# A fused attention, gate and routing pipeline: wider softmax-sum pieces, bf16 high parts written by ScalarE, a prefix in three steps, and a second table of places for the last three iterations

## The reference, cut to what matters

```
# x: (16, 128, 32, 32): 16 images of 1024 pixels, 128 channels
xn   = batchnorm(x)                                   # running statistics
qkv  = qkv_w @ xn + qkv_b                             # 4 heads of 32
attn = softmax(q^T k / sqrt(128)) over 1024 keys
x    = x + out_w @ (attn v) + out_b
t    = tokens(x)                                      # (16, 1024, 128)
z    = layernorm(t)
k, v = per-head norm of z (8 heads of 16, std with n-1)
t    = t + z @ (k^T v / N) + z                        # linear attention
z2   = layernorm(t)
p    = softmax(z2 @ gate_w + gate_b); the two largest of 8 experts
t    = t + sum over the two of p_e * (gelu(z2 @ W1_e + b1_e) @ W2_e + b2_e)
out  = images(t)
```

## Time and profile before

| what | value |
|---|---|
| median of 3 runs | 2252.08 us (2238.56 to 2256.55) |
| profiled execution | 2246.34 us, of which the span of instructions 2244.6 us |
| mean granted TensorE clock | 0.863 |
| phase 1 with attention | from 50 us to 1530 us of the span |
| iterations 16 to 18, tables | 1530 us to 1660 us |
| phases 2 and 3 | 1660 us to 2244.6 us |

### The profile page before, as it was taken

The page is one execution under the profiler, slowest core; times in us unless marked ns, Lnnn a source line. Parts: engine busy times, 40 slices in busy tenths (PEclk is TensorE's granted clock), DMA queues, the critical chain, the costliest instruction groups (busy, mean ns, idle before and its releaser), DMA issues.

```text
span 2244.6 us, 38139 instructions
## 1 busy us (share of the span) xinstructions
PE 1754.7 (78%) x11103; PEld 884.2 (39%) x11256; DVE 1379.7 (61%) x3701; ACT 1071.3 (48%) x1898; POOL 1434.8 (64%) x1779
## 2 busy tenths in 40 slices
PE   5999898897888989798898978885337677777744
PEld 2233333332333333333333333333326566566632
DVE  5677878686776768677686866754434333333345
ACT  1565655555455555545455555452115444444432
POOL 1777587875968678596877769676335555555530
PEclk8999999998988999799898999896568888887865
DMA  2220220211202022120202112010323333322259
GB/s 64 57 57 12 55 81 17 76 37 51 77 14 84 15 76 53 38 77 21 76 13 75 47 44 73 6 38 31 101 76 119 107 115 96 93 76 75 74 150 319
DMA packets 130824, 155.20 MB, mean 69 GB/s; under 512 B 19678, under 2 KB 93170, under 8 KB 130688
## 3 DMA queue, kind: packets, MB, share of 16 engines
q1 hardware_dynamic: 113408, 117.76, 18.9%
q0 software_dynamic: 16896, 35.69, 4.7%
q10 hardware_dynamic: 384, 0.00, 0.0%
HBM read 65.03 MB, written 55.84 MB: 54 GB/s over the span
## 4 chain that ended last, share of the span: by engine, by line
PE 49%; issue 14%; DVE 12%; another core or an unknown queue 8%; POOL 6%; ACT 5%; SPq 4%; DMA 1%; DVEq 0%; ACTq 0%; POOLq 0%
PE psum L1573 8%; PE psum L1620 7%; PE psum L1593 7%; PE psum L1683 6%; DVE rowmax L1198 5%; PE psum L1670 5%; PE psum L1554 3%; PE psum L1421 3%; POOL probs L624 2%; PE psum L1428 2%; PE psum L1576 2%; PE psum L1659 2%; PE psum L1458 1%; POOL arena L624 1%
## 5 line engine op out<-in xcount | busy, mean ns | idle before, releaser
L1198 DVE TENSOR_REDUCE rowmax<-psum 128x1 f32<-128x512 f32 x1024 | 670.1, 681 | 304.3 <-PE psum L1620 184.9
L1620 PE MATMUL psum<-arena 128*128 128x512 bf16 x872 | 332.9, 405 | 103.8 <-DVE rowmax L1198 81.1
L797 ACT ACTIVATE probs<-psum 128x1024 f32<-128x1024 f32 x256 | 251.1, 1021 | 209.7 <-PE psum L1576 203.5
L797 ACT ACTIVATE arena<-psum 128x1024 f32<-128x1024 f32 x256 | 252.7, 1021 | 179.8 <-PE psum L1576 176.6
L610 POOL DMA_INDIRECT sorted_scratch<-rows,slot_idx x256 | 251.1, 981 | 91.9 <-issue 69.6
L1620 PEld LDWEIGHTS psum<-arena 128*128 128x128 bf16 x1024 | 92.5, 101 | 550.0 <-DVE rowmax L1198 384.9
L1573 PE MATMUL psum<-qk 32*128 32x512 f32 x2048 | 300.6, 657 | 7.9 <-ACT probs L797 4.3
L1683 PE MATMUL psum<-probs 128*128 x1088 | 186.4, 326 | 100.5 <-ACT probs L866 100.4
L624 POOL TENSOR_TENSOR probs<-probs 128x256 f32<-128x256 f32 x352 | 243.7, 729 | 16.5 <-PE psum L1593 13.5
L624 POOL TENSOR_TENSOR arena<-arena 128x256 f32<-128x256 f32 x352 | 243.9, 728 | 13.5 <-PE psum L1593 10.9
L1683 PEld LDWEIGHTS psum<-probs 128*128 128x128 f32 x1088 | 174.9, 236 | 128.9 <-issue 121.6
(11 more groups left out here) (203 smaller groups left out, 2794.3 us busy)
## 6 DMA issues: line engine op xcount, KB each, us to landing
arena<-part SPq DMA_DIRECT2D x256, 128.0 KB, 2.8
qk<-sorted_scratch SPq DMA_DIRECT2D x136, 144.0 KB
probs<-y_scratch SPq DMA_DIRECT2D x64, 256.0 KB, 5.1
x_in<-in_x_dram SPq DMA_DIRECT2D x16, 512.0 KB, 3.5
x_res<-in_x_dram SPq DMA_DIRECT2D x16, 512.0 KB
t_scratch<-t SPq DMA_DIRECT2D x16, 512.0 KB
arena<-t_scratch SPq DMA_DIRECT2D x8, 1024.0 KB
out_dram<-probs SPq DMA_DIRECT2D x32, 256.0 KB, 5.3
```

Source lines behind the costliest of these rows:

```text
L797: a.activation(group[:, 2 * i:2 * i + 2, :].rearrange("p s n -> p (s n)"), st_pair[i], ACT.Exp, scale=float(C) ** -0.5).then_inc(exp_done, 1)
L1198: v.tensor_reduce(rowmax[:, half, kh, h, j:j + 1], ps[:, :], AX.X, ALU.max)\
L1620: t_.matmul(ps[:, :], qs1[:, par, h, qb * P:(qb + 1) * P], ks1[:, par, h, kh * HALF:(kh + 1) * HALF], start=True, stop=True)\
```

## The change

1. SUM_PARTS goes from 8 to 4: each pair of exponential blocks is added in four instructions of 512 columns, not in eight of 256.
2. The high part of q and k is written by ScalarE from PSUM, ahead of the float32 copy that it already wrote; GpSimd keeps the low part. For image 0, two high parts move from DVE to ScalarE.
3. The Gram matrix's four instructions after PE's product (usum, kvw[0], udiag, kcc) move from DVE to ScalarE, in the piece "gram"; the head mask is multiplied into vrow once at the start, and the identity is added in the second product, so that `kv_product` has one instruction less (three after usum, not four).
4. The running count over blocks is made in three instructions of 64 columns (sums of two, of four, of eight) from padded tiles `chosen`, `two_of`, `four_of`. Two slot products become one instruction, two slot sums too.
5. In AT: zT1 goes from quarter 27 to 24, ss from 25 to 23, the third pair of z from 20 to 19, prefix to (27, 28, 31).
6. Iterations 16 to 18 take their places from a second table, AFTER. Against AT it has, among others: proj1 13, gram 27, usum 31, z (17, 19, 19, 19), ss 23, square 24, heads 27, u 31, scatter (11, 13, 14, 16, 19, 19, 22, 26), z2 (12, 13, 15, 15), ln0 15, ln1 1, norm1 1, kv1 to kv3 at 0, 2, 5, slot_numbers 6, prefix (30, 31, 31), stats0a and stats0b 14, 15, deviations0 18, gsum 19.
7. In the last image's second half only the pairs 0 and 1 are summed by GpSimd; PE takes the blocks of pairs 2 and 3 one by one.

```diff
-    PAIRS, SUM_PARTS = 4, 8
+    PAIRS, SUM_PARTS = 4, 4
     SUMMED = (0, 1, 2, 3)
+    LAST_SUMMED = (0, 1)
+    def summed_at(n):
+        return LAST_SUMMED if n == 2 * B - 1 else SUMMED
+    def table(pair, p):
+        return AT if 2 * pair + p < B else AFTER
...
+        chosen = sb("chosen", [P, 1 + BLK, E])
+        two_of = sb("two_of", [P, 2 + BLK, E])
+        four_of = sb("four_of", [P, 4 + BLK, E])
...
                 pool.wait_ge(raw_ready, 4 * b + c + 1)
-                g.tensor_copy(part[:, 0, which, cols], qk[:, par, which, cols]).then_inc(high_ready, 1)
-                pool.wait_ge(high_ready, parts_made(b, c))
+                pool.wait_ge(high_ready, 4 * b + c + 1)
                 g.tensor_tensor(part[:, 1, which, cols], qk[:, par, which, cols], part[:, 0, which, cols],
                                 ALU.subtract).then_inc(mid_ready, 1)
...
+                    if b > 0 and name == "q0":
+                        for h in range(NH):
+                            act.wait_ge(stacked1[1 - par][h], 16 * STACK1_DMAS * ((b - 1) // 2 + 1))
+                    a.activation(part[:, 0, which, cols], ps[:, :], ACT.Identity,
+                                 bias=bqk[:, which:which + 1]).then_inc(high_ready, 1)
                     a.activation(qk[:, par, which, cols], ps[:, :], ACT.Identity,
                                  bias=bqk[:, which:which + 1]).then_inc(raw_ready, 1)
...
+                elif name == "gram":
+                    ps = from_shared(name, pair, p)
+                    a.activation(usum[:, :], ps[:, C:C + 1], ACT.Copy).then_inc(gram_out, 1)
+                    a.activation(kvw[:, 0, :], ps[:, 0:C], ACT.Copy, scale=kcol[:, 0:1]).then_inc(gram_out, 1)
+                    act.wait_ge(gram_out, 3 * b + 1)
+                    a.activation(udiag[:, :], ident[:, :], ACT.Copy, scale=usum[:, :]).then_inc(udiag_ready, 1)
+                    a.activation(kcc[:, :], usum[:, :], ACT.Identity, scale=kcol[:, 0:1], bias=kb_n[:, :])\
+                     .then_inc(gram_out, 1)
...
-                    v.scalar_tensor_tensor(kvw[:, 3, :], vrow[:, 1, :], kcc[:, :], kvw[:, 2, :],
+                    dve.wait_ge(gram_out, 3 * b + 3)
+                    v.scalar_tensor_tensor(kvw[:, 3, :], vrow[:, 1, :], kcc[:, :], ident[:, :],
                                            ALU.mult, ALU.add).then_inc(kv_step, 1)
                 else:
-                    dve.wait_ge(kv_step, 6 * b + 6)
-                    v.tensor_tensor(kvw[:, 4, :], kvw[:, 3, :], headmask[:, :], ALU.mult).then_inc(bd_ready, 1)
-                    dve.wait_ge(bd_ready, 2 * b + 1)
-                    v.tensor_tensor(bd[:, :], kvw[:, 4, :], ident[:, :], ALU.add).then_inc(bd_ready, 1)
+                    dve.wait_ge(kv_step, 3 * b + 3)
+                    v.tensor_tensor(bd[:, :], kvw[:, 2, :], kvw[:, 3, :], ALU.add).then_inc(bd_ready, 1)
...
+                    if k == 0:
+                        ins = v.tensor_tensor(two_of[:, 2:, :], chosen[:, 1:, :], chosen[:, 0:BLK, :], ALU.add)
+                    elif k == 1:
+                        ins = v.tensor_tensor(four_of[:, 4:, :], two_of[:, 2:, :], two_of[:, 0:BLK, :], ALU.add)
                     else:
-                        dve.wait_ge(prefix_step, 8 * b + k)
-                    v.tensor_tensor(before[:, k + 1, :], before[:, k, :], lg[:, 8, k, :], ALU.add)\
+                        ins = v.tensor_tensor(before[:, 1:, :], four_of[:, 4:, :], four_of[:, 0:BLK, :], ALU.add)
...
-                for c in range(2):
-                    v.tensor_reduce(slot_of[:, c, :], slot[:, 1 + c, :, :], AX.X, ALU.add).then_inc(slot_step, 1)
+                v.tensor_reduce(slot_of[:, :, :], slot[:, 1:3, :, :], AX.X, ALU.add).then_inc(slot_step, 1)
...
                 for i in pairs:
-                    if i in SUMMED:
+                    if i in summed_at(n):
                         pe.wait_ge(summed, len(SUMMED) * n + SUMMED.index(i) + 1)
                     else:
                         pe.wait_ge(probs_used, PAIRS * n + i + 1)
-                    groups = (2 * i,) if i in SUMMED else (2 * i, 2 * i + 1)
+                    groups = (2 * i,) if i in summed_at(n) else (2 * i, 2 * i + 1)
```

More of the change, by code:

```diff
@@ L89, in conv_attention_hybrid_kernel, with order @@
     }
-    SHARED = {n: (AT[n], LAG[n]) for n in LAG}
-    PAIRS, SUM_PARTS = 4, 8
+    AFTER = dict(AT)
+    AFTER.update({'rank': 1, 't2_0': 8, 't2_1': 10, 'proj0': 11, 'proj1': 13, 'z2T0': 17, 'z2T1': 18, 'logits': 19, 'zT0': 23, 'zT1': 24, 'gram': 27, 'usum': 31, 'values1': 1, 'ln1': 1, 'z2': (12, 13, 15, 15), 'gexp': 20, 'ln0': 15, 'z': (17, 19, 19, 19), 'square': 24, 'ln_heads': 26, 'norm1': 1, 'd16': 20, 'u': 31, 'scatter': (11, 13, 14, 16, 19, 19, 22, 26), 'kv1': 0, 'kv2': 2, 'kv3': 5, 'slot_numbers': 6, 'stats1a': 9, 'stats1b': 10, 'deviations1': 13, 'gate': (20, 23, 23, 23, 24, 24, 24, 24, 25, 25, 26, 26, 26, 26, 27, 29), 'prefix': (30, 31, 31), 'stats0a': 14, 'stats0b': 15, 'deviations0': 18, 'gsum': 19, 'ss': 23, 'heads': 27, 'den1': 5})
+    PAIRS, SUM_PARTS = 4, 4
     SUMMED = (0, 1, 2, 3)
-    ORDER = sorted(SHARED, key=lambda n: SHARED[n][0])
+    LAST_SUMMED = (0, 1)
[3 more added lines that the diff above has]
+        return AT if 2 * pair + p < B else AFTER
+    def order(pair, p):
+        return sorted(LAG, key=lambda n: table(pair, p)[n])
     OTHER_WEIGHTS_AT = max(AT[n] for n in ("q0", "k0", "q1", "k1")) + 1
@@ L135, in row_target, with denominators_at @@
         return (0, 1, r) if r < 4 else (1, 0, r - 4) if r < 8 else (1, 1, 0)
-    DENOMINATORS = tuple((SHARED[n][0], SHARED[n][1], int(n[3])) for n in ORDER if n[:3] == "den")
+    def denominators_at(pair, p):
+        return tuple((table(pair, p)[n], LAG[n], int(n[3])) for n in order(pair, p) if n[:3] == "den")
     DEN_STEPS = ((0, (0, 1)), (1, (2, 3)))
@@ L638, in iteration @@
                         for half in (0, 1):
[L639 to L642, removed]
+                            when = 16 * half + at["sum"][i]
+                            lag = -(when // QUARTERS)
+                            if q == when % QUARTERS and in_range(lag, pair, p):
+                                b = image(lag, pair, p)[0]
+                                if i in summed_at(2 * b + half):
+                                    sum_pair(b, half, i)
                     if in_range(1, pair, p):
                         b, _, par = image(1, pair, p)
-                        if q == AT["split"][0]:
+                        if q == at["split"][0]:
                             _, prp, parp = image(0, pair, p)
@@ L1528, in previous @@
             def previous(name, pair, p):
-                mine = ORDER
+                mine = order(pair, p)
                 i = mine.index(name)
@@ L1628, in iteration @@
                             values(b, par, sv, 1 if j == 1 else 0)
-                    for first, lag, half in DENOMINATORS:
+                    for first, lag, half in denominators_at(pair, p):
                         for later, pairs in DEN_STEPS:
```

177 lines of the change are left out of this document (90 added, 87 removed).

## The result

| | before | after |
|---|---|---|
| median of 4 runs each | 2246.77 us (2238.56 to 2256.55) | 2347.59 us (2342.01 to 2350.81) |
| profiled execution, its own time and span | 2246.34, 2244.6 us | 2342.01, 2340.2 us |
| mean granted clock | 0.863 | 0.859 |

The ratio is 1.0444, 95% interval 1.0392 to 1.0497: 101 us slower, where 2247 us had been forecast with a range of 2213 to 2283.

A forecast was written before the change was run, and what follows sets the result against it. Steady iterations were taken as bound by TensorE's work plus stalls, the tail by engine-to-engine latencies. Terms +24 - 17 + 0 - 10 = -3 us against 2246.3 gave 2243; forecast median 2247, range 2213 to 2283.

The forecast's parts named there:

- sums of 512 columns: GpSimd's pair sums over VectorE's chain in quarter 17: each later chain instruction waits 0.6 us more; +24 us, 0 to 33.
- the slower rival: Quarter 17's lock at full rate (+33), A not ending earlier, den1 bare (+9), tail -7: +35, 2285 us; chance 0.21.
- The longer chain of `deviations`: Quarter 17, four small VectorE instructions under a GpSimd sum: three later ones wait about 1.25 us, chain 1.8 us longer.
- The rate of 3.5 us for 1.9: Quarter 17: 1.9 us more of VectorE went with 3.5 us more of the iteration; 3.3 us each in 10 iterations.
- High parts by ScalarE: Quarters 2 to 6: casts move from GpSimd to ScalarE, DMA burst ends 1.4 us earlier in 12 iterations; -17 us.
- The arithmetic on the burst's start: GpSimd's last low part, and with it the burst of DMAs into `arena`, comes about 1.4 us earlier.
- den1's wait: Sums over keys wait for ScalarE's copy of q1: 0.69 us later, some 0.6 us an iteration, about 1.1 us in profile.
- A: Stall in quarter 14, some 5 us in twelve iterations: an engine's progress hangs on DMA queues until the burst has drained.
- Gram products, prefix and moved places: VectorE instructions removed or moved to ScalarE, places shifted: hidden by TensorE's matmuls, 0 us; remaining two-input instructions -5 to +10.
- The exponential behind the gram piece: Quarter 28: ScalarE's second exponential queues behind the gram piece, and quarter 30's scores need it; 0, at worst +10 us.
- Own tail: After the last scores: unsummed pairs 2 and 3, less TensorE idling, earlier gsum, shorter ScalarE and prefix work; -10 us, -5 to -14.

The follow-up runs named there:

- the fourth experiment: The changed kernel, four pieces a sum, without the second table of places and with all pairs of the last half summed; ratio 1.0529 to the kernel before.

## Why the prediction was wrong

**The step that failed** is in the part on sums of 512 columns: "the two engines take turns by whole instructions", from which the wait of any VectorE instruction was bounded by one piece (+0.6 us each), the term by 0 to 33 us, and the slower rival by the same mechanism. The later members of a `deviations` chain, which ask again right behind their own last turn, did get one at the end of each piece, 38 of 38 under the sums of the kernel after. Another instruction can be passed over at every boundary until GpSimd's queue has a pause. The kernel after lost 104 us by that alone (1.0444 against 0.9979 with the pause behind each piece), which no case of the prediction held.

The evidence stood in the earlier trace rows: 3.54 and 3.50 us of one small instruction in the chain, until the end of the sum. I read them as a fixed price of a few iterations ("those which already wait for the whole sum don't get worse") and used them only as a measure of what a longer chain costs. I didn't ask why those instructions did not get a turn at the sum's next piece, when their three neighbours did, nor what the longest run of GpSimd instructions is that a passed-over one could be held through: two sums and a norm back to back, in quarters 28 and 29.

The rule of the Trainium skill's page "SBUF — State Buffer", section "Who interferes with whom" (a port pair locked for the whole instruction) agrees with the trace for the chain in quarter 17: 0.65 us at 256 columns, 1.13 and 1.20 at 512. In quarter 28 the measurement goes beyond it, by 10.6 us through nine instructions, and the measurement decides.

**The other terms.** The longer chain of `deviations` was seen as forecast (1.13 to 1.20 us a step). Its price was forecast at +24 with 0 to 33. With pauses behind each piece, so that nobody is passed over, four pieces give 0.9979 and eight 0.9853, 28 +- 12 us between them, by ratios from two chips and with all other turns in it. That agrees with the size; that it is all quarter 17's is not shown. The rate of 3.5 us for 1.9, taken from three iterations against seven, had a weak base: in the run of eight pieces with pauses, where no chain is held, the steady iterations still differ by 8 us (90.8 to 98.7).

High parts by ScalarE, forecast -17: measured +6 (-2 to +13) alone, and no difference with eight pieces. The arithmetic on the burst's start was right in direction (2.2 us earlier where I had 1.4), and den1's wait came as forecast, 1.1 us. The assumption that failed is that A begins where it did and only ends earlier. It moved with the burst and took in a copy that had been ahead of it, and so it gave nothing back.

Gram products, prefix and moved places, forecast 0: with eight pieces and no own tail the change has all of these and the high parts, and stands at 1.0000 +- 0.0045; less the +6 of the high parts that is -6 +- 12. Not told from 0. The exponential behind the gram piece didn't show up as a wait.

Own tail, forecast -10 (-5 to -14): 11 us in the last turn, and 25 +- 12 or 39 +- 18 by the ratios. The last turn did get shorter, as forecast; the size may be too small.

With these sizes the sum for four pieces is 104 + 28 + 6 - 6 - 11 to 25, 107 to 121 us, where 101 were measured; within the errors of the terms that closes. It is no independent proof, since the 104 is measured from the kernel after itself. What it tests is the rest: -11 to -25 by the single terms, -25 to -39 by the three runs with eight pieces and all else of the change.

## What to carry to other kernels

A small instruction whose time is many times its work is a wait, also when the profile counts it as busy. Ask of the longest one which queue's end it waits for, and how long that queue can get elsewhere in the kernel; the mean of its neighbours is no bound. When VectorE and GpSimd both work in SBUF, look for long unbroken runs of GpSimd instructions and either put a pause in them or try another length of piece, and measure, because the length works in both directions. And before crediting the earlier start of a stall, see what stands just ahead of it that it will take in.

## What the runs showed of the hardware

A VectorE instruction that adds two parts of SBUF tiles, 64 columns wide, was held 10.6 us behind nine GpSimd instructions, and 12.4 to 14.0 us behind pieces of 128 columns. It ended 0.08 to 0.09 us after the last of them in every one of these 24 cases. With 256-column pieces the same instruction at the same place was served at the end of the piece that it met in 12 of 12 iterations of one run (0.34 to 0.41 us), whether it came 0.5 or 2.5 us into the run of pieces, and in 10 of 12 of another. But 256 columns are no safe length: the kernel before has the four waits of 3.1 to 3.7 us at the head of `deviations`.

What decides at a boundary stays open. It is not the arrival alone: at 512 columns four_of was passed over wherever it came, from 0.01 to 0.76 us into a piece (12 of 12 iterations of the fourth experiment), while other instructions that came 0.2 to 1.2 us into one were served at its end (all 27 first members of the `deviations` and kv chains that met a sum in the kernel after; in the kernel before with four pieces, 2 of 13 first members of `deviations` were passed over, 2.7 and 3.3 us). With a pause behind each piece, all 105 VectorE instructions with two SBUF inputs that began while a piece ran were served at that piece's end. Which GpSimd instruction follows, or what else runs in quarter 28, was not varied alone.
